# A Mamba and mixture-of-experts layer on one core: a quarter of the scan's input products move from VectorE to ScalarE and TensorE

## The chip, the core and the metric

The kernel runs on one core of a Trainium2 chip. The core has TensorE (PE in the profile, its weight loads PEld), VectorE (DVE), ScalarE (ACT), GpSimd (POOL) and a sync engine (SP) that issues DMAs. The metric is the device time in microseconds. Three runs of the kernel before took 1241.63, 1243.11 and 1251.92 us.

## The reference

For 8 sequences of 512 tokens with 128 features, x is normalised and fed to two branches, whose results are added to x:

```python
xn = _layernorm(x, axis=-1)
x = x + attn(xn) + ffn(xn)
# attn: two directions (the second on the reversed sequence), each
u = silu(causal_conv(x_part) + b)                 # 256 channels
delta = softplus(dt_proj @ x_dbl[:r] + dt_bias)   # (d, l)
dA  = exp(delta[d, l] * A[d, n])                  # 16 states n
dBx = delta[d, l] * Bm[n, l] * u[d, l]
h   = scan over l of  h = dA * h + dBx
y   = sum over n of h * Cm[n, l]  + D * u;  y * silu(z)
# attn result: (forward + backward) @ out_proj
# ffn: top 4 of 16 experts per token, softmax of the 4 logits as weights,
hidden = gelu(x @ w1[e].T + b1[e]);  hidden @ w2[e].T + b2[e]
```

All is float32.

## The kernel before, in words

**Preparation.** The first 275 us or so normalise the tokens, route them to experts (DVE), scatter them to tiles of 256 rows in DRAM (POOL), and compute for each of the 8 batches (sequences) delta, du = delta * u, the gate, and Bm and Cm, all stored to DRAM. Bm is kept as three bf16 parts in `parts`, so that a bf16 matmul with 0/1 weights `sel` sums them to the f32 value.

**The scan loop.** Channels lie on the 128 partitions; there are 256 channels, so NH = 2 halves h, and ND = 2 directions d. A batch has PAIRS = 32 steps q. Step q handles half h = q % 2 of direction d = q // 2 % 2, for the pair of states 2g and 2g + 1 with g = q // 4 (j = 0 and 1). For each of the 64 (q, j) of a batch:

- PE broadcasts row n of Bm over all partitions into one of four PSUM banks `b_ps` (L1007; called a fill).
- DVE multiplies the bank by du in place (`dbx`, L1235, the input product).
- ACT computes the decay exp(delta * A) (L829) into a ring of 8 steps.
- DVE runs the scan over 512 positions (L1257), into the ring `state` of 8 steps.

Then for each q the state times Cm (a 128x1024 product, the state product) is done by POOL (L666), or by DVE (L1245) for the steps of `vector_pairs(b)`: 4 steps in the first batch, 5 in the last and one in the others. PE adds the products up by transposing them into `y_ps` (L954, eight transposes a step, `sum_states`), four steps later (SUM_LAG).

**The experts beside it.** 10 tiles a batch are worked off in the same loop, at fixed steps (`EVENTS`, with `FIRST` and `LAST` for the first and last batch). Of tile j, T transposes the rows (L968), U0 and U1 are the first matmuls (L975), D is the second with its bias (L982 and L984, the bias as a matmul of one row of ones), G and O turn and project the gated output of the batch before. They share two PSUM banks `m_ps`; ACT empties them (L769, L773, L779, L782) at a step of its own that is 4 to 6 later (`EMPTY_STEP`), and runs the gelus in two bursts of five a batch, at its steps 5 and 21 (L797, with table loads before and after). POOL sends each finished tile to DRAM by scatter-add (`send`, L651, two indirect DMAs) one step after its D.

**The order.** Each engine runs one program in order, written out by hand, with semaphores between them. ACT's decays can run 8 steps ahead of DVE's scans. PE's fill for tau = 2q + j waits for the scan of tau - 4. PE does at step q: two fills, the events, the sum of step q - 4. The scan of q waits for the sum of q - 8. SP loads Cm rows, weights and the next batch's data in a fixed order, behind waits on the products.

```python
for j in range(2):
    tau = 2 * q + j
    if tau + 1 < DECAYS:
        dbx(tau + 1)
    ...
    nc.vector.tensor_tensor_scan(state[:, q % H_RING, j, way], ...)
```

Of the kernel before, what the change touches and what calls it, by code (L numbers as in the profile page):

```python
# [6 lines left out]
BF16 = mybir.dt.bfloat16  # L7
# [6 lines left out]
P = 128  # L14
# [45 lines left out]
FIRST_VECTOR = (1, 4, 7, 10)  # L60
VECTOR = (16,)
LAST_VECTOR = (16, 19, 22, 25, 28)
# [7 lines left out]


# [19 lines left out]
GATE_STEP, MIX_STEP = 3, 16  # L91
# [4 lines left out]
FIRST = [[] for _ in range(PAIRS)]  # L96
# [14 lines left out]
for _k, (_q, _j, _before) in enumerate(LAST_D):  # L111
    LAST[_q].append(("D", _j, 1 if _q < LAST_U[-1] else _k % 2, _before))
for _j, _q in enumerate(LAST_T):
    LAST[_q].append(("T", _j, 0, False))
for _j, _q in enumerate(LAST_U):
    LAST[_q] += [("U0", _j, 1, False), ("U1", _j, 0, False)]
# [42 lines left out]
def uses_before(b, m):  # L159

    if isinstance(b, int) and b == 0:
        return 0
    if isinstance(b, int) and b == BATCH:
        return uses_before(BATCH - 1, m) + sum(e[2] == m for q in LAST for e in q)
    return sum(e[2] == m for q in EVENTS for e in q) * b - sum(e[2] == m and e[3] for q in EVENTS for e in q)

# [51 lines left out]
def build_kernel(nc, x_in, consts_in, chan_in, inw_in, xproj_in, dtw_in, outw_in,  # L218
                 route_in, b2_in, w1_in, w2_in, out):
    with ExitStack() as ctx:  # L220
# [33 lines left out]

        delta = sb("delta", [P, 2, DH, L])
# [10 lines left out]
        b2 = sb("b2", [P, W_RING, D])  # L266
        ones = sb("ones", [P, P])
# [5 lines left out]
        ARENA = (DA_RING + H_RING + C_RING) * 2 * L + MPB * FC * S  # L273
# [3 lines left out]
        def carve(n):  # L277
# [5 lines left out]
        decay = carve(DA_RING * 2 * L).rearrange("p (r j l) -> p r j l", r=DA_RING, j=2)  # L283
        state = carve(H_RING * 2 * L).rearrange("p (r j l) -> p r j l", r=H_RING, j=2)
        c_rows = carve(C_RING * 2 * L).rearrange("p (r j l) -> p r j l", r=C_RING, j=2)
        hidden = carve(MPB * FC * S).rearrange("p (t f s) -> p t f s", t=MPB, f=FC)
# [54 lines left out]
        xpad = carve(NH * PADL).rearrange("p (h l) -> p h l", h=NH)  # L341
        v = by_q(carve(DH * L))
        u = [by_q(carve(DH * L)) for _ in range(2)]
        xdbl = by_d(carve(ND * L))
# [16 lines left out]
        b_ps = ps[:, 0:B_RING, :]  # L361
# [11 lines left out]
            late_in1 skip_in0 skip_in1 decay_ready b_ready dbx_done scan_done prod_done v_prod_done summed y_free m0_ready m0_free m1_ready m1_free gelu_done  # L373
            mixed_out mixed_in sp_step pool_step acc_ready out_done"""
# [27 lines left out]
        def _(sp):  # L402
# [6 lines left out]
            for dst, src in ((chan[:, :, :], chan_in), (inw, inw_in), (xproj, xproj_in), (dtw[BR:BR + NR], dtw_in),  # L409
# [3 lines left out]
                with nc.allow_non_contiguous_dma(reason="one row of biases"):  # L413
                    sp.dma_start(dst, src).then_inc(s["wts_in"], 16)

# [44 lines left out]
            def read_down(tile, slot):  # L460
# [3 lines left out]
                sp.dma_start(b2[0:1, slot, :], b2_in[bass.ds(e, 1)]).then_inc(w2_in_s[slot], 16)  # L464
# [13 lines left out]
            def read_first():  # L478

                sp.wait_ge(s["scattered"], 16 * NT * TOPK)  # L480
                for j in range(W_RING):
# [23 lines left out]

            store_gate(0)
# [11 lines left out]
            def read_c(b, r):  # L518
                g, d = r // ND, r % ND
                src = c_d[bass.ds(b, 1), d, 2 * g:2 * g + 2, :].rearrange("e j l -> e (j l)")  # L520
                sp.dma_start(c_rows[:, r % C_RING, :, :].rearrange("p j l -> p (j l)"),
# [26 lines left out]
            def batch(b, par):  # L548
                last = isinstance(b, int) and b == BATCH - 1
                for q in range(PAIRS + 2):  # L550
                    if q == 0 and not last:

                        wait(sp, s["decay_ready"], DECAYS * b)
                        wait(sp, s["dbx_done"], DECAYS * b)
                        wait(sp, s["b_ready"], DECAYS * b)
# [30 lines left out]
            sp.wait_ge(s["mixed_out"], 16 * (BATCH - 1))  # L586
            half = BATCH // 2
# [27 lines left out]
        def _(pool):  # L615
# [4 lines left out]
            nc.gpsimd.iota(xn[:, :, D].bitcast(I32), [[L, BATCH], [1, TPB]], base=UNUSED, channel_multiplier=TPB).then_inc(s["ids_ready"], 1)  # L620

# [61 lines left out]
        def _(act):  # L683
# [75 lines left out]
            for b in range(BATCH):  # L759
                prepare(b)  # L760
            act.wait_ge(s["decay_free"], 1)

            def empty(b, q):
# [576 lines left out]
```

## Time and profile before

| | |
|---|---|
| median of three runs | 1243.11 us |
| profiled execution, its time | 1242.92 us |
| its span | 1240.0 us |
| instructions | 20530 |
| busy: DVE / PE / POOL / ACT | 1131.2 / 996.3 / 985.2 / 809.9 us |
| first and last scan start | 279.9, 1200.1 us |
| PE weight loads busy | 748.6 us |

Times in the rows are microseconds from the start of the span, unless marked ns. A busy engine is one with an instruction in flight; two records of one engine can overlap, since the next begins before the last has quite ended. What an instruction costs in a full queue is therefore the distance from start to start. Idle time is put down to what ended it.

### The profile page before, as it was taken

The page shows a single profiled execution, that of the slowest core. Times are in us where ns is not written, and L with a number is a line of the kernel's source. Part 1 is how long each engine was busy: PE and PEld are TensorE (multiplying, and loading weights), DVE is VectorE, ACT ScalarE, POOL GpSimd, SP SyncE. Part 2 cuts the span into 40 slices and gives each one's busy share as a digit, 9 for nine tenths or more (in the row PEclk, how much of TensorE's full clock was granted, in tenths as well). Part 3 has the DMA queues.
Part 4 walks back from the last instruction along what each step waited for, and adds up shares of the span by engine and source line. Part 5 has one row for each costly group of instructions (what it writes and reads, how often), then busy time and mean ns, then how long its engine had stood idle before and what let it go on. Part 6 is the DMA issues. An engine that isn't in the chain of part 4 may idle for free.

```text
span 1240.0 us, 20530 instructions
## 1 busy us (share of the span) xinstructions
PE 996.3 (80%) x5548; PEld 748.6 (60%) x5636; DVE 1131.2 (91%) x1516; ACT 809.9 (65%) x1367; POOL 985.2 (79%) x540
## 2 busy tenths in 40 slices
PE   5277888645789888988998889899889888998972
PEld 5133333213567677776777677677667776777762
DVE  6876888759999999999999999999999999998972
ACT  2047877855677676767677676667676776767520
POOL 1077868763489989998999898799989998997673
PEclk9988787776999999999999998999999999999886
DMA  9824455486556767576676667566765666655545
GB/s 318 299 83 168 164 202 183 174 295 219 158 158 152 196 184 186 157 214 172 146 210 175 178 153 215 141 177 164 210 184 146 206 177 169 171 145 151 127 102 148
DMA packets 150908, 222.52 MB, mean 179 GB/s; under 512 B 35597, under 2 KB 97373, under 8 KB 145893
## 3 DMA queue, kind: packets, MB, share of 16 engines
q1 hardware_dynamic: 123652, 202.12, 51.7%
q0 software_dynamic: 27136, 19.02, 10.8%
q8 instruction: 49, 0.80, 0.3%
q14 instruction: 71, 0.57, 0.2%
HBM read 159.71 MB, written 65.50 MB: 182 GB/s over the span
## 4 chain that ended last, share of the span: by engine, by line
issue 37%; DVE 32%; PE 14%; POOL 7%; DMA 5%; ACT 3%; DVEq 1%; another core or an unknown queue 1%; SPq 0%; POOLq 0%; ACTq 0%
DVE ps L1235 20%; DVE arena L1257 7%; POOL arena L666 4%; POOL acc_d L651 3%; DMA acc_d<-yrows,tags 3%; PE ps L909 2%; PE ps L885 2%; PE ps L917 2%; PE ps L894 2%; PE ps L975 1%; PE ps L954 1%; PE ps L982 1%; PE ps L867 1%; ACT arena L829 1%; PE ps L1007 1%
## 5 line engine op out<-in xcount | busy, mean ns | idle before, releaser
L666 POOL TENSOR_TENSOR arena<-arena 128x1024 f32<-128x1024 f32 x241 | 608.2, 2832 | 85.3 <-DVE arena L1257 73.9
L1257 DVE TENSOR_TENSOR_SCAN arena<-arena,ps 128x512 f32<-128x512 f32 x512 | 617.7, 1208 | 0.0
L829 ACT ACTIVATE arena<-delta,a_neg 128x511 f32<-128x511 f32 x512 | 336.9, 719 | 39.2 <-DVE arena L1257 28.3
L1235 DVE TENSOR_TENSOR ps<-du,ps 128x512 f32<-128x512 f32 x512 | 344.1, 673 | 14.2 <-remote 9.8
L651 POOL DMA_INDIRECT acc_d<-yrows,tags x160 | 252.3, 1577 | 45.0 <-issue 36.7
L954 PE MATMUL ps<-ident,arena 128*128 128x128 f32 x2048 | 275.1, 279 | 0.0
L1007 PE MATMUL ps<-parts,sel 128*128 128x512 bf16 x425 | 154.9, 392 | 118.2 <-DVE arena L1257 101.5
L954 PEld LDWEIGHTS ps<-ident,arena 128*128 128x128 f32 x2048 | 236.9, 144 | 17.4 <-issue 0.8
L982 PE MATMUL ps<-w,arena 128*128 128x128 f32 x1280 | 184.6, 288 | 6.0 <-ACT yrows L779 5.6
L633 POOL DMA_INDIRECT slots_d<-arena,pos x128 | 155.8, 1217 | 42.1 <-issue 40.7
L779 ACT ACTIVATE yrows<-ps,tags 128x128 f32<-128x128 f32 x160 | 49.9, 363 | 197.6 <-PE ps L984 148.9
L982 PEld LDWEIGHTS ps<-w,arena 128*128 128x128 f32 x1280 | 160.1, 194 | 26.1 <-issue 8.0
L773 ACT ACTIVATE arena<-ps,w 128x256 f32<-128x256 f32 x320 | 131.4, 471 | 46.4 <-PE ps L975 41.8
L975 PE MATMUL ps<-rowsT,w 128*128 128x256 f32 x640 | 157.5, 390 | 1.6 <-issue 0.9
L1007 PEld LDWEIGHTS ps<-parts,sel 128*128 128x128 bf16 x512 | 50.2, 98 | 164.0 <-DVE arena L1257 149.1
L975 PEld LDWEIGHTS ps<-rowsT,w 128*128 128x128 f32 x640 | 124.6, 196 | 26.6 <-issue 3.5
L797 ACT ACTIVATE arena<-arena 128x1024 f32<-128x1024 f32 x80 | 81.1, 1053 | 0.2
L984 PE MATMUL ps<-b,ones 1*128 1x128 f32 x320 | 78.6, 325 | 0.0
L1150 DVE SCALAR_TENSOR_TENSOR arena<-arena,chan 128x512 f32<-128x512 f32 x96 | 64.3, 743 | 0.0
L984 PEld LDWEIGHTS ps<-b,ones 1*128 1x128 f32 x320 | 47.6, 186 | 19.7 <-issue 0.9
L630 POOL COPY arena<-gates 128x32 f32<-128x32 f32 x4 | 7.2, 1808 | 64.5 <-DVE pos L1123 56.1
L885 PE MATMUL ps<-arena 128*128 128x256 f32 x64 | 28.6, 625 | 33.5 <-ACT arena L701 26.9
(122 smaller groups left out, 831.3 us busy)
## 6 DMA issues: line engine op xcount, KB each, us to landing
arena<-c_d SPq DMA_DIRECT2D x128, 512.0 KB
w<-w_dram SPq DMA_DIRECT2D x80, 258.0 KB
w<-w_dram SPq DMA_DIRECT2D x80, 256.0 KB
rows<-slots_d SPq DMA_DIRECT2D x80, 130.0 KB
slots_d<-delta SPq DMA_DIRECT2D x5, 2015.0 KB, 20.1
delta_d<-arena SPq DMA_DIRECT2D x8, 1024.0 KB
du_d<-delta SPq DMA_DIRECT2D x8, 1024.0 KB
delta<-delta_d SPq DMA_DIRECT2D x8, 1024.0 KB, 6.9
```

What stands on the lines that cost most here:

```text
L633: pool.indirect_dma_start(slots_d, bass.IndirectOffsetOnAxis(ap=pos[:, t * TOPK + k:t * TOPK + k + 1], axis=0), xn[:, t, :], None).then_in ...
L651: pool.indirect_dma_start(acc_d, bass.IndirectOffsetOnAxis(ap=tags[:, j, a, 0:1].bitcast(I32), axis=0), yrows[:, j % W_RING, a, :], None, ...
L666: nc.gpsimd.tensor_tensor(state[:, q % H_RING], state[:, q % H_RING], c_rows[:, r % C_RING], ALU.mult).then_inc(s["prod_done"], 1)
L773: last = nc.scalar.activation(hidden[:, j, c, :], bank[:, f * S:(f + 1) * S], ACT.Identity, bias=w1[:, j % W_RING, FF + c:FF + c + 1])
L829: nc.scalar.activation(decay[:, q % DA_RING, j, lo:lo + L - 1], delta[:, par, dh, lo:lo + L - 1], ACT.Exp, scale=a_neg[:, dh, 2 * g + j:2 ...
L954: last = nc.tensor.matmul(y_ps[:, h, t * P:(t + 1) * P], state[:, q % H_RING, j, t * P:(t + 1) * P], ident[:, :], is_transpose=True, start ...
L975: last = nc.tensor.matmul(bank[:, f * S:(f + 1) * S], w1[:, slot, c * P:(c + 1) * P], rowsT[:, :], start=True, stop=True)
L982: nc.tensor.matmul(bank[:, a * P:(a + 1) * P], hidden[:, j, c, a * P:(a + 1) * P], w2[:, slot, c, :], start=c == 0, stop=False)
L984: last = nc.tensor.matmul(bank[:, a * P:(a + 1) * P], ones[0:1, :], b2[0:1, slot, :], start=False, stop=True)
L1007: nc.tensor.matmul(b_ps[:, tau % B_RING, :], sel[:, 2 * g + j, :], parts[:, par, d, :], start=True, stop=True).then_inc(s["b_ready"], 1)
L1235: nc.vector.tensor_tensor(bank, du[:, par, tau // 2 % DH, :], bank, ALU.mult).then_inc(s["dbx_done"], 1)
L1257: nc.vector.tensor_tensor_scan(state[:, q % H_RING, j, way], decay[:, q % DA_RING, j, way], b_ps[:, tau % B_RING, way], 0.0, ALU.mult, ALU ...
```

## The change

Of the input products, those with d = 0 and j = 1 (`scaled(q, j)`, 16 of 64 a batch) are no longer made by DVE. du of a batch's forward direction is transposed once (positions on partitions) into `duT`, and so is Bm into `bT`. For each group g ACT multiplies four 128x256 blocks of `duT` by the per-partition scalar `bT[:, t, n]` into `scaled_du` (a ring of 2), and PE transposes them into the PSUM bank, four transposes a fill. The transposing of the next batch is two new kinds of events, X (du, one half each) and Y (Bm), at steps 18 and 19.

Where a fill is still a broadcast row, it is made once for both halves: for even q DVE reads the row in one bank of its j and writes the product to the other; for odd q it works in place. Five fills are left for four steps (`FILLS`), six input products on DVE (`DBX`). The order of DVE's instructions is written out for groups of four steps.

State products on DVE become 3, 3 and 8 in the first, the middle and the last batch. Expert bias b2 is split into three bf16 parts by POOL at the start, stored to DRAM, and added by a bf16 matmul of three rows. `hidden` shrinks from ten slots to five (two more in the last batch lie in `delta`). The steps of T and D in the last batch shift a little.

```diff
-FIRST_VECTOR = (1, 4, 7, 10)
-VECTOR = (16,)
-LAST_VECTOR = (16, 19, 22, 25, 28)
+FIRST_VECTOR = (1, 4, 7)
+VECTOR = (8, 16, 24)
+LAST_VECTOR = (13, 16, 18, 20, 22, 24, 26, 28)
...
+def scaled(q, j):
+    return q // NH % ND == 0 and j == 1
+FILLS = [(q, j) for q in range(PAIRS) for j in (1, 0) if scaled(q, j) or q % NH == 0]
+DBX = [(q, j) for g in range(0, PAIRS, DH) for q, j in ((g, 0), (g + 1, 0), (g + 2, 1), (g + 2, 0), (g + 3, 0), (g + 3, 1))]
+def fill_of(q, j):
+    return 1 + FILLS.index((q, j) if scaled(q, j) else (q - q % NH, j))
...
+SCAN_ORDER = [(0, 1), (0, 0), (1, 1), (1, 0), (2, 1), (2, 0), (3, 0), (3, 1)]
+def scans_to(q, j):
+    return 2 * DH * (q // DH) + SCAN_ORDER.index((q % DH, j)) + 1
+PROD_RING = 2
+PROD_AHEAD = 2
+SCALED = PAIRS // DH
...
+EVENTS[18] += [("X", 0, 0, False), ("Y", 0, 1, False)]
+EVENTS[19].insert(0, ("X", 1, 0, False))
...
-LAST_T = [0, 3, 5, 8, 10, 12, 15, 17, 20, 22]
-LAST_U = [1, 4, 6, 9, 11, 13, 16, 18, 21, 23]
-LAST_D = [(2, 5, True), (5, 6, True), (7, 7, True), (10, 8, True), (12, 9, True), (17, 0, False), (19, 1, False),
+LAST_T = [0, 2, 4, 7, 9, 12, 15, 17, 20, 22]
+LAST_U = [2, 4, 6, 9, 11, 13, 16, 18, 21, 23]
+LAST_D = [(1, 5, True), (3, 6, True), (5, 7, True), (8, 8, True), (10, 9, True), (17, 0, False), (19, 1, False),
...
@@ SP
-                sp.dma_start(b2[0:1, slot, :], b2_in[bass.ds(e, 1)]).then_inc(w2_in_s[slot], 16)
+                sp.dma_start(b2[0:3, slot, :], b2_d[bass.ds(e, 1)].rearrange("e k d -> (e k) d")).then_inc(w2_in_s[slot], 16)
...
+            sp.wait_ge(s["b2_split"], 4)
+            sp.dma_start(b2_d.rearrange("e k d -> e (k d)"), b2_parts.rearrange("e k d -> e (k d)")).then_inc(s["b2_out"], 16)
             store_gate(0)
...
@@ POOL
+            pool.wait_ge(s["b2_in"], 16)
...
+            nc.gpsimd.tensor_copy(b2_parts[:, 0, :], b2_f).then_inc(s["b2_split"], 1)
...
@@ ACT
+            act.wait_ge(s["turn_ps"], 3)
+            act.wait_ge(s["du_ready"], ND * (BATCH - 1))
+            for h in range(NH):
+                nc.scalar.copy(duT[:, 0, :, h * P:(h + 1) * P], ps[:, h, :].rearrange("p (t c) -> p t c", t=TPB)).then_inc(s["turned"], 1)
+            nc.scalar.copy(bT[:, 0, :, :].rearrange("p t n -> p (t n)"), ps[:, 2, 0:TPB * NS]).then_inc(s["turned"], 1)
+            def scale(b, g, par):
+                n = 2 * g + 1
+                before = fill_of(DH * ((g - PROD_RING) % SCALED) + NH - 1, 1)
+                wait(act, s["b_ready"], len(FILLS) * (b if g >= PROD_RING else b - 1) + before)
+                for t in range(TPB):
+                    last = nc.scalar.activation(scaled_du[:, g % PROD_RING, t, :], duT[:, par, t, :], ACT.Identity,
+                                                scale=bT[:, par, t, n:n + 1])
+                last.then_inc(s["scaled"], 1)
...
+                    if (q + PROD_AHEAD) % DH == 0:
+                        g = (q + PROD_AHEAD) // DH
+                        if g < SCALED:
+                            scale(b, g, par)
+                        elif not (isinstance(b, int) and b == BATCH - 1):
+                            for what, j, m in (("X", 0, 0), ("X", 1, 0), ("Y", 0, 1)):
+                                bank_emptied(act, s, b, what, j, m)
+                            scale(b + 1, 0, 1 - par)
...
@@ PE
+            def turn_du(bank, par, h):
+                for t in range(TPB):
+                    last = nc.tensor.transpose(bank[:, t * P:(t + 1) * P], du[:, par, h, t * P:(t + 1) * P], ident[:, :])
+                return last
...
+            pe.wait_ge(s["delta_ready"], ND * BATCH)
+            pe.wait_ge(s["turned"], 3)
...
-                            last = nc.tensor.matmul(bank[:, a * P:(a + 1) * P], ones[0:1, :], b2[0:1, slot, :], start=False, stop=True)
+                            last = nc.tensor.matmul(bank[:, a * P:(a + 1) * P], ones[0:3, :], b2[0:3, slot, :], start=False, stop=True)
...
+                    for j in (1, 0):
+                        if (q, j) in FILLS:
+                            wait(pe, s["scan_done"], DECAYS * b + scans_to(q - 2, j))
+                            if scaled(q, j):
+                                pe.wait_ge(s["scaled"], SCALED * b + g + 1)
+                                bank = b_ps[:, ROW[q, j], j, :]
+                                for t in range(TPB):
+                                    last = nc.tensor.transpose(bank[:, t * P:(t + 1) * P],
+                                                               scaled_du[:, g % PROD_RING, t, h * P:(h + 1) * P], ident[:, :])
+                            else:
+                                last = nc.tensor.matmul(b_ps[:, ROW[q + 1, j], j, :], sel[:, 2 * g + j, :], parts[:, par, d, :],
+                                                        start=True, stop=True)
+                            last.then_inc(s["b_ready"], 1)
...
@@ DVE
+                def dbx(q, j):
+                    dve.wait_ge(s["b_ready"], len(FILLS) * b + fill_of(q, j))
+                    if q % NH == 0:
+                        wait(dve, s["scan_done"], DECAYS * b + scans_to(q - 1, j))
+                    b_row = b_ps[:, ROW[q - q % NH + 1, j], j, :]
+                    nc.vector.tensor_tensor(b_ps[:, ROW[q, j], j, :], du[:, par, q % DH, :], b_row, ALU.mult)\
+                        .then_inc(s["dbx_done"], 1)
...
+                for q in range(0, PAIRS, DH):
+                    dbx(q, 0)
+                    product(q - 1)
+                    scan(q, 1)
+                    scan(q, 0)
+                    dbx(q + 1, 0)
+                    product(q)
+                    scan(q + 1, 1)
+                    scan(q + 1, 0)
+                    dbx(q + 2, 1)
+                    product(q + 1)
+                    dbx(q + 2, 0)
+                    scan(q + 2, 1)
+                    dbx(q + 3, 0)
+                    scan(q + 2, 0)
...
+                    dbx(q + 3, 1)
+                    product(q + 2)
+                    scan(q + 3, 0)
+                    scan(q + 3, 1)
```

## Rows read from the trace of the kernel before

**Rows 1.** The page, busy microseconds, share of the span and instructions of each engine.

```profile
PE 996.3 (80%) x5548; PEld 748.6 (60%) x5636; DVE 1131.2 (91%) x1516; ACT 809.9 (65%) x1367; POOL 985.2 (79%) x540
```

**Rows 2.** Stretches: length, busy of PE, PEld, DVE, ACT, POOL; granted clock, DMA share, GB/s.

```profile
406.60:518.40 111.80, 97.73 (x641) 80.26 (x652) 111.77 (x133) 80.77 (x152) 104.10 (x52) 1.00 0.68 180
...
743.80:860.50 116.70, 103.79 (x645) 83.49 (x653) 114.25 (x133) 81.39 (x154) 102.72 (x52) 0.96 0.67 175
```

**Rows 3.** Timeline of DVE in a middle batch: start, length, engine, line, operation, operands.

```profile
638.92 1.21 DVE L1257 TENSOR_TENSOR_SCAN arena<-arena,ps 128x512 f32<-128x512 f32 x1
640.04 0.67 DVE L1235 TENSOR_TENSOR ps<-du,ps 128x512 f32<-128x512 f32 x1
...
664.54 1.21 DVE L1257 TENSOR_TENSOR_SCAN arena<-arena,ps 128x512 f32<-128x512 f32 x1
```

**Rows 4.** Timeline of DVE at the end of the first batch.

```profile
393.49 2.32 DVE L1257 TENSOR_TENSOR_SCAN arena<-arena,ps 128x512 f32<-128x512 f32 x2
```

**Rows 5.** The group of L1245, then timelines of DVE and POOL around three of its instructions.

```profile
L1245 DVE TENSOR_TENSOR arena<-arena 128x1024 f32<-128x1024 f32 x15 | 24.6, 1643 | 1.0
...
679.57 1.23 DVE L1245 TENSOR_TENSOR arena<-arena 128x1024 f32<-128x1024 f32 x1
...
795.00 2.94 POOL L666 TENSOR_TENSOR arena<-arena 128x1024 f32<-128x1024 f32 x1
795.61 3.42 DVE L1245 TENSOR_TENSOR arena<-arena 128x1024 f32<-128x1024 f32 x1
...
1188.34 3.27 DVE L1245 TENSOR_TENSOR arena<-arena 128x1024 f32<-128x1024 f32 x1
```

**Rows 6.** Timeline of the last batch and the tail; in brackets the idle time before.

```profile
1128.43 2.77 PE L994 MATMUL ps<-outw,gatedT 128*128 128x128 f32 x16 [3.45 <-ACT gatedT L782]
...
1133.45 0.70 DVE L1235 TENSOR_TENSOR ps<-du,ps 128x512 f32<-128x512 f32 x1 [4.15 <-remote]
...
1200.41 0.62 ACT L779 ACTIVATE yrows<-ps,tags 128x128 f32<-128x128 f32 x2 [9.95 <-DMA acc_d<-yrows,tags]
```

**Rows 7.** Timeline of POOL in a middle batch: a send, three products, the next send.

```profile
645.53 1.60 POOL L651 DMA_INDIRECT acc_d<-yrows,tags  x1 [0.17 <-issue]
647.44 1.57 POOL L651 DMA_INDIRECT acc_d<-yrows,tags  x1 [0.30 <-issue]
648.44 7.59 POOL L666 TENSOR_TENSOR arena<-arena 128x1024 f32<-128x1024 f32 x3
656.20 1.58 POOL L651 DMA_INDIRECT acc_d<-yrows,tags  x1 [0.16 <-issue]
```

**Rows 8.** Timeline of PE and ACT at a batch's step 18, behind the gelu burst.

```profile
679.80 1.15 PE L982 MATMUL ps<-w,arena 128*128 128x128 f32 x8
...
680.20 1.33 ACT L829 ACTIVATE arena<-delta,a_neg 128x511 f32<-128x511 f32 x2
682.99 0.62 ACT L779 ACTIVATE yrows<-ps,tags 128x128 f32<-128x128 f32 x2 [1.45 <-PE ps L984]
...
685.71 1.70 ACT L773 ACTIVATE arena<-ps,w 128x256 f32<-128x256 f32 x4 [0.89 <-PE ps L975]
```

**Rows 9.** Groups of one middle batch (518.4 to 630.3): busy, mean ns, idle before.

```profile
L666 POOL TENSOR_TENSOR arena<-arena 128x1024 f32<-128x1024 f32 x32 | 81.2, 2885 | 3.1 <-DVE arena L1257 3.1
...
L954 PE MATMUL ps<-ident,arena 128*128 128x128 f32 x256 | 33.7, 275 | 0.0
...
L984 PE MATMUL ps<-b,ones 1*128 1x128 f32 x40 | 9.7, 321 | 0.0
L779 ACT ACTIVATE yrows<-ps,tags 128x128 f32<-128x128 f32 x20 | 6.2, 363 | 23.1 <-PE ps L984 18.6 <-issue 4.4
```

**Rows 10.** Timeline of PE: two fills in a row.

```profile
649.14 0.59 PE L1007 MATMUL ps<-parts,sel 128*128 128x512 bf16 x2
```

**Rows 11.** Timeline of ACT at the start of the scan loop.

```profile
276.66 12.33 ACT L829 ACTIVATE arena<-delta,a_neg 128x511 f32<-128x511 f32 x20 [8.51 <-DVE arena L1198]
```

**Rows 12.** Stretches, as in rows 2, of seven microseconds in the fifth batch.

```profile
758.00:765.00 7.00, 6.78 (x24) 5.64 (x25) 5.34 (x7) 2.57 (x6) 6.44 (x4) 0.55 0.74 182
```

More of the change, by code:

```diff
@@ L69, in vector_pairs @@
     return VECTOR
+def scaled(q, j):
[4 more added lines that the diff above has]
+    return 1 + FILLS.index((q, j) if scaled(q, j) else (q - q % NH, j))
+ROW = {}
+for _j in range(2):
+    _last = 1
+    for _q in range(0, PAIRS, NH):
+        ROW[_q, _j], ROW[_q + 1, _j] = (1 - _last, _last) if scaled(_q, _j) else (_last, 1 - _last)
+        _last = ROW[_q + 1, _j]
+    assert _last == 1 and NH == 2
+SCAN_ORDER = [(0, 1), (0, 0), (1, 1), (1, 0), (2, 1), (2, 0), (3, 0), (3, 1)]
[4 more added lines that the diff above has]
+SCALED = PAIRS // DH
 SUM_LAG = 4
@@ L373, in build_kernel @@
             late_in1 skip_in0 skip_in1 decay_ready b_ready dbx_done scan_done prod_done v_prod_done summed y_free m0_ready m0_free m1_ready m1_free gelu_done
+            b2_in b2_split b2_out turn_ps turned scaled
             mixed_out mixed_in sp_step pool_step acc_ready out_done"""
@@ L586, in _ @@
             sp.wait_ge(s["mixed_out"], 16 * (BATCH - 1))
+            for j in (GROUP, GROUP + 1):
+                m = [e[2] for step in LAST for e in step if e[:2] == ("D", j) and not e[3]][0]
+                bank_written(sp, s, BATCH - 1, "D", j, m)
             half = BATCH // 2
@@ L782, in empty @@
                         last = nc.scalar.copy(gatedT[:, j, :], bank)
+                    elif what == "X":
+                        last = nc.scalar.copy(duT[:, 1 - par, :, j * P:(j + 1) * P], bank.rearrange("p (t c) -> p t c", t=TPB))
+                    elif what == "Y":
+                        last = nc.scalar.copy(bT[:, 1 - par, :, :].rearrange("p t n -> p (t n)"), bank[:, 0:TPB * NS])
                     else:
@@ L988, in besides @@
                             last = nc.tensor.transpose(bank[:, t * P:(t + 1) * P], gated[:, j, t, :], ident[:, :])
+                    elif what in ("X", "Y"):
+                        pe.wait_ge(s[f"early_in{1 - par}"], 48 * (i + par) + 48)
+                        last = turn_du(bank, 1 - par, j) if what == "X" else turn_b(bank, 1 - par)
                     else:
@@ new lines, in dbx, with scan @@
+                def dbx(q, j):
[5 more added lines that the diff above has]
+                        .then_inc(s["dbx_done"], 1)
+                def scan(q, j):
+                    dve.wait_ge(s["decay_ready"], DECAYS * b + 2 * q + j + 1)
+                    if scaled(q, j):
+                        dve.wait_ge(s["b_ready"], len(FILLS) * b + fill_of(q, j))
+                    else:
+                        dve.wait_ge(s["dbx_done"], len(DBX) * b + DBX.index((q, j)) + 1)
+                    wait(dve, s["summed"], PAIRS * b + q - H_RING + 1)
+                    way = slice(None) if q % DH < NH else slice(None, None, -1)
+                    nc.vector.tensor_tensor_scan(state[:, q % H_RING, j, way], decay[:, q % DA_RING, j, way],
+                                                 b_ps[:, ROW[q, j], j, way], 0.0, ALU.mult, ALU.add).then_inc(s["scan_done"], 1)
```

125 lines of the change are left out of this document (72 added, 53 removed).

## The prediction

> **What bounds the kernel now.** I read the page's busy line first: VectorE (DVE) is busy 91% of the span, more than any other engine [rows 1]. The table by stretches then separates the stages: from 406.6 us on, a batch of the scan loop takes 111.9 us, in which DVE is busy 111.8, POOL 104.1, PE 99 and ACT 81 [rows 2]. DVE waits for nobody in such a batch, so what a batch costs is what DVE's instructions cost. The timeline of DVE gives their real price, from start to start, as records overlap: 15 pairs of an input product (L1235) and a scan (L1257) lie between the first and the last row shown, 25.62 us or 1.708 a pair; the scan's part is 1.12 to 1.13 and so the product's 0.58 [rows 3]. 64 pairs are 109.3, one state product on DVE 1.15, two gate products 1.2: 111.7 of the 111.9. The profiled execution took 1242.92 us, its span 1240.0, and the median of the three runs is 1243.11, so the sum made against the profiled one holds for the median too.
>
> **DVE, what goes.** A quarter of the input products (those of d = 0, j = 1: 16 of 64 a batch) leave DVE: 16 x 0.58 = 9.3 us a batch. The new order puts scan behind scan; two adjacent scans are recorded once a batch end, 2.32 us for both, so the second starts 1.11 after the first, no dearer than 1.13 [rows 4]. An even q now reads its row in one bank and writes another; the nearest row is the in-place product at 0.58. It could cost a little more or less; I take the same, since the shape and memories are those of L1235.
>
> **DVE, what comes.** State products move from POOL to DVE: 3 a batch in place of 1, 3 in place of 4 in the first, 8 in place of 5 in the last. One alone takes 1.23 us (slot 1.15), as at 679.57 where POOL was issuing a send. At 795.61 it took 3.42: POOL was inside its own product from 795.00 to 797.94, and the DVE product ended 1.1 us after that. At 1188.34, 3.27 in the same way. The mean of the 15 is 1.643 [rows 5]. So the slot lies between 1.15 and 3.35. The clean ones fell on sends or on an idle POOL; with three a batch at places not tied to a send and POOL inside a product 0.64 of the time (29 x 2.34 of 107), half of a product's 2.34 is the mean wait: 0.64 x 1.17 = 0.75, so 1.9 a slot. The Trainium skill, page "SBUF — State Buffer", section "SBUF: two separate sides", says that a DVE instruction with two inputs in SBUF and a GpSimd one that reads SBUF take one port pair as an exclusive lock for the whole instruction. The trace agrees, with 3.42 against 1.23 us. Without a lock, each product at 1.15, the sum would be 1185; the rule speaks against the change's extra products, not against its scaled ones (one input of L1235 is PSUM, and it never stretched).
>
> **The sum for DVE.** A middle batch: 48 x 0.58 + 64 x 1.125 = 99.8; gate 1.2; three products 5.7; 106.7 in all. For brief stalls of a now tighter loop I add 0.8 (0 to 4 would be the bounds, the latter from the one stall of the last batch [rows 6]), so 107.5 against 111.9: 4.4 saved, x 6 = 26. First batch: 9.3, and one product fewer among idle or light POOL, +0.8, less 0.6 as the first fill now stands behind four transposes: 9.5. Last batch: 9.3 + 8.6 (the five old products: 1.2, 1.2, 1.2, 1.7, 3.3) - 15.2 (eight at 1.9) = 2.7. The tail after 1201 us hangs on the scatter-adds: ACT waits 9.95 us for a send to land before it may fill the next slot [rows 6]; nothing of it changes, and it moves with the last batch. 26 + 9.5 + 2.7 = 38: 1242.9 - 38 = 1205.
>
> **POOL.** Three products make 7.02 us between the ends of the last send and of the third product, 2.34 each; a send takes the other 3.61 of a 10.63 us cycle [rows 7]. Now 31 x 2.34 + 10 x 3.61 = 108.6 a batch; after, 29 x 2.34 + 36.1 = 104.0, plus up to 3 x 1.15 where DVE holds what POOL wants: 104 to 107.4. It is nearly level with DVE. Sends come in stretches, so POOL falls behind by some 4 us over eight steps and gets it back at the DVE products; PE's sum is four steps behind, which covers about 6.
>
> **ACT.** Added are 32 ACTIVATEs of 128x256 a batch. Four such from PSUM take 1.70, 0.41 each; from SBUF they lie between 0.41 and the 0.61 of a 511-wide decay, two of which take 1.33 [rows 8]; I take 0.41: 13.1, and 1.4 for the turned copies. 81 + 14.5 = 95.5 of 107.5. It fits beside DVE because ACT's 23 us of idle before L779 in a batch are mostly waits for PE's D, which ACT reaches early [rows 9]. Its cover gone, each us above costs one us of loop. The scale is issued two steps ahead and its ring of two is refilled against transposes five steps older, so it waits for nobody.
>
> **PE.** Two fills in a row take 0.59, 0.3 each [rows 10]; 40 fewer save 12. L954's 256 transposes keep PE busy 33.7 us, 0.13 each [rows 9]; 64 more are 8.4, and with a start-up for each group of four 10. The biases in f32 take 9.7 a batch [rows 9]; in bf16 with three rows something between 0 and that; I take 4.7: 5 saved. X and Y add 12 small ones, 1.6. Net 5 less: 94 of 107.5. But PE is in order, and X and Y put two new waits for ACT at steps 18 and 19 behind which the fills of step 20 stand. PE began D of step 18 at 679.80, ACT was through its gelu burst at 680.20 and emptied D at 682.99 [rows 8]. From there: Y, X copies, X, U0, U1, two sums and the fills of 20 come to about 9 us from the start of D; DVE has 6 scans, 5 input products and one state product to do, 11.5. It just fits.
>
> **Start and queues.** Transposing batch 0 and the three copies fall in the idle time before the first decays, 8.5 us of ACT up to 276.66 [rows 11], which wait for DVE's last preparation; some 4 us of work there, cost 0, at most 3 if the load of du comes late. The split of b2 is four small POOL instructions ahead of its wait for pos, which DVE computes much later: 0. On SP's queue the store of b2 and the extra waits (b2_split ahead of the first gate store, products 8 and 24) are passed long before the rest is due: 0, at most 1.
>
> **Rivals.** (a) POOL sets the pace: 107.4 plus the 3.1 us that it still waits for scans in a batch [rows 9] is 110.5, 1.4 saved x 6, + 12: 1222. For it: 104 to 107 against 106.7 leave no room. (b) The new waits park PE as ACT's late copy did in the last batch: PE waited 3.45 us, DVE 4.15 [rows 6]. Once in each of 7 batches: 1205 + 29 = 1234. (c) Slower: ACT becomes the bound, because its waits for PE's D don't shrink as it falls behind. Then a batch is 95.5 + 23.1 = 118.6, + 6.7 x 6 - 9.5: 1273. It decides once more than 16.4 of the 23.1 us stay. Against it: ACT is up to eight steps ahead, and such waits end at PE's time. (d) Products hit POOL's sends and nothing stalls: 104.5 a batch, 7.4 x 6 + 10.5 + 8.7: 1179. (e) PE's clock. Between 758 and 765 us PE was granted 0.55, a fall to its lower level, 1.2 GHz, right after ordinary busy work; that batch took 116.7 [rows 2, 12]. One such stretch in each of 7 batches: 1205 + 33 = 1238. The Trainium skill, "TensorE: Matmul & The Clock Gate", part 4, says that transposes don't count as busy for the clock, and this change swaps matmuls for transposes. The trace is against it so far: a steady batch with 256 transposes of L954 alone holds 1.00 [rows 2, 9]. (f) The change does less than it says, DVE still running 512 input products: 1243. The diff leaves six of eight in each group of four steps, so this gets 2%.
>
> **Chances.** Forecast 0.50, (a) 0.14, (b) 0.09, (c) 0.11, (d) 0.11, (e) 0.03, (f) 0.02. A measurement of this kernel can tell about 1%, 12 us: faster is below 1231, slower above 1255. Faster: 0.50 + 0.14 + 0.11 less some for overlap of (a) with the border: 0.73. Within: 0.15. Slower: 0.12. The bounds of the product slot alone give 1179 (1.15) and 1242 (3.35); (a) and (b) lie between, (c) is left out. Range 1180 to 1238.
>
> **What would show it.** Right: scans in a middle batch stay unbroken, gates 107 to 108 us apart, 384 input products on DVE, 29 state products of mean 1.7 to 2.2 us, PE's waits at fills for scans still there. Wrong: DVE idle before L1257's or L1235's successors released by PE (b), by ACT decays (c), or scans held by sums behind POOL (a); granted clock under 0.9 in a middle batch (e).

## The result: 1% slower, and the profile after

The changed kernel took 1252.1 us in the median of five runs (1248.43 to 1265.39) against 1241.6 for the kernel before; the ratio is 1.0107, with a 95% interval of 1.006 to 1.0154. The forecast of 1205 us was wrong. Run again beside its variants it took 1255.42 against 1244.61, ratio 1.0097 (1.0064 to 1.013). Now and then a run of a kernel takes 1.5% or more longer than its shortest; where that matters below, its time is named beside the others.

The profiled execution of the changed kernel is the slowest of its five, 1265.39 us with a span of 1263.5, so I use it for the pattern and not for the sum. Its busy line answers [rows 1]:

```profile
PE 981.4 (78%) x5764; PEld 781.2 (62%) x5764; DVE 1087.3 (86%) x1402; ACT 915.4 (72%) x1647; POOL 874.1 (69%) x530
```

DVE did get rid of work: 44 us less. But it is now busy 86% of the span, no longer 91%. The table by stretches, cut at the gate products as in [rows 2], shows the same in a middle batch:

```profile
409.10:523.10 114.00, 96.78 (x668) 84.42 (x668) 107.69 (x118) 94.03 (x187) 89.39 (x49) 0.96 0.64 174
...
873.50:989.50 116.00, 98.26 (x668) 85.47 (x668) 107.81 (x119) 94.07 (x188) 89.37 (x49) 0.94 0.65 173
```

DVE's work of a batch is 107.7 us, where I had 106.7. The six middle batches take 114.0 to 119.7, so 6 to 12 us of each are waits; the first batch of [rows 2] had none. POOL's 89.4 is far below my 104. The page's groups say who waits, and for whom (line, engine, operands, count; then busy and mean ns; then the idle time before and its releasers):

```profile
L747 POOL TENSOR_TENSOR arena<-arena 128x1024 f32<-128x1024 f32 x227 | 486.9, 2241 | 219.4 <-DVE arena L1389 208.4
L1389 DVE TENSOR_TENSOR_SCAN arena<-arena,ps 128x512 f32<-128x512 f32 x512 | 600.9, 1205 | 1.2 <-ACT arena L932 1.2
L1377 DVE TENSOR_TENSOR ps<-du,ps 128x512 f32<-128x512 f32 x384 | 254.7, 678 | 50.3 <-PE ps L1146 47.9
...
L854 ACT ACTIVATE arena<-arena 128x256 f32<-128x256 f32 x256 | 108.7, 497 | 36.8 <-PE ps L1143 36.8
...
L1096 PE MATMUL ps<-ident,rows 128*128 128x128 f32 x160 | 35.4, 306 | 85.2 <-ACT arena L872 84.8
```

L1389 is the scan, L1377 the input product, L1146 and L1143 the fills (row and transposes), L854 the new scaling, L1096 the transposing T of an expert tile, L872 ACT's emptying of U0 and U1. Read upwards it is a chain: ACT stands before the scaling until PE has made certain transposes, PE stands 85 us before T until ACT has emptied U1, and DVE stands before its input products until PE has filled. Also DVE waits at the gate products (L1365):

```profile
873.47 0.67 DVE L1365 TENSOR_TENSOR gated<-ps,gate 128x512 f32<-128x512 f32 x1
...
877.84 0.69 DVE L1365 TENSOR_TENSOR gated<-ps,gate 128x512 f32<-128x512 f32 x1 [3.71 <-PE ps L1082]
```

The timeline around step 29 of a batch shows how one such meeting goes (start, length; idle before in brackets):

```profile
849.40 0.60 PE L1143 MATMUL ps<-ident,arena 128*128 128x128 f32 x4
...
850.04 1.71 ACT L854 ACTIVATE arena<-arena 128x256 f32<-128x256 f32 x4 [2.87 <-PE ps L1143]
...
851.65 1.54 ACT L872 ACTIVATE arena<-ps,w 128x256 f32<-128x256 f32 x4
...
853.25 0.44 PE L1096 MATMUL ps<-ident,rows 128*128 128x128 f32 x2 [3.25 <-ACT arena L872]
...
854.86 1.29 DVE L1377 TENSOR_TENSOR ps<-du,ps 128x512 f32<-128x512 f32 x2 [2.05 <-PE ps L1146]
```

ACT had been idle for 2.87 us when PE made the transposes of step 29 (L1143); only then could it scale (1.6 us) and only then empty U1 (1.6 us). PE needs that bank for T of the same step 29, so it stood 3.25 us, which is the two together. DVE ran out of filled rows and stood 2.05. This is the dearest of several meetings: in the whole trace ACT waits before the scaling 16 times, twice in a middle batch, but PE waits before T behind L872 34 times. So a part of PE's 84.8 us has no wait of ACT's before it.

### The profile page after: what moved, and what is told of

It reads as the page before. It is cut to its first block, busy times and chain, and to the rows that moved or that the text cites. A ratio compares the mean times of both kernels' runs of the same rounds, so it can differ in the third digit from the quotient of the medians.

```text
span 1263.5 us, 21454 instructions
## 1 busy us (share of the span) xinstructions
PE 981.4 (78%) x5764; PEld 781.2 (62%) x5764; DVE 1087.3 (86%) x1402; ACT 915.4 (72%) x1647; POOL 874.1 (69%) x530
## 4 chain that ended last, share of the span: by engine, by line
issue 17%; PE 16%; ACT 15%; POOL 10%; DVE 4%; DMA 3%; DVEq 0%; SPq 0%; ACTq 0%; POOLq 0%
POOL arena L747 5%; POOL acc_d L732 5%; PE ps L1111 5%; PE ps L1082 4%; ACT arena L932 4%; ACT arena L854 3%; ACT arena L872 3%; PE ps L1103 3%; DVE arena L1389 2%; ACT arena L900 2%; DMA acc_d<-yrows,tags 2%; PE ps L1143 2%; DVE ps L1377 1%; ACT L932 1%; PE ps L1146 1%
## 5 line engine op out<-in xcount | busy, mean ns | idle before, releaser
L747 POOL TENSOR_TENSOR arena<-arena 128x1024 f32<-128x1024 f32 x227 | 486.9, 2241 | 219.4 <-DVE arena L1389 208.4
L1389 DVE TENSOR_TENSOR_SCAN arena<-arena,ps 128x512 f32<-128x512 f32 x512 | 600.9, 1205 | 1.2 <-ACT arena L932 1.2
L1377 DVE TENSOR_TENSOR ps<-du,ps 128x512 f32<-128x512 f32 x384 | 254.7, 678 | 50.3 <-PE ps L1146 47.9
L1082 PE MATMUL ps<-ident,arena 128*128 128x128 f32 x2048 | 285.8, 285 | 2.9 <-POOL arena L747 2.9
L1082 PEld LDWEIGHTS ps<-ident,arena 128*128 128x128 f32 x2048 | 245.5, 148 | 16.7 <-POOL arena L747 3.4
L1111 PEld LDWEIGHTS ps<-w,arena 128*128 128x128 f32 x1248 | 169.7, 208 | 22.6 <-ACT yrows L878 7.2
L878 ACT ACTIVATE yrows<-ps,tags 128x128 f32<-128x128 f32 x160 | 49.6, 361 | 128.4 <-PE ps L1113 95.2
L872 ACT ACTIVATE arena<-ps,w 128x256 f32<-128x256 f32 x312 | 125.8, 468 | 19.7 <-PE ps L1103 18.5
L854 ACT ACTIVATE arena<-arena 128x256 f32<-128x256 f32 x256 | 108.7, 497 | 36.8 <-PE ps L1143 36.8
L1143 PE MATMUL ps<-ident,arena 128*128 128x128 f32 x512 | 84.5, 292 | 24.3 <-DVE arena L1389 18.5
L1096 PE MATMUL ps<-ident,rows 128*128 128x128 f32 x160 | 35.4, 306 | 85.2 <-ACT arena L872 84.8
L1146 PE MATMUL ps<-parts,sel 128*128 128x512 bf16 x192 | 71.3, 415 | 25.4 <-DVE arena L1389 25.4
L1143 PEld LDWEIGHTS ps<-ident,arena 128*128 128x128 f32 x512 | 64.3, 151 | 28.5 <-DVE arena L1389 21.8
L1096 PEld LDWEIGHTS ps<-ident,rows 128*128 128x128 f32 x160 | 19.8, 149 | 99.9 <-ACT arena L872 86.6
```

What stands on the lines that cost most here:

```text
L747: nc.gpsimd.tensor_tensor(state[:, q % H_RING], state[:, q % H_RING], c_rows[:, r % C_RING], ALU.mult).then_inc(s["prod_done"], 1)
L854: last = nc.scalar.activation(scaled_du[:, g % PROD_RING, t, :], duT[:, par, t, :], ACT.Identity, scale=bT[:, par, t, n:n + 1])
L872: last = nc.scalar.activation(hidden[hidden_slot(b, j)][:, c, :], bank[:, f * S:(f + 1) * S], ACT.Identity, bias=w1[:, j % W_RING, FF + c: ...
L1082: last = nc.tensor.matmul(y_ps[:, h, t * P:(t + 1) * P], state[:, q % H_RING, j, t * P:(t + 1) * P], ident[:, :], is_transpose=True, start ...
L1111: nc.tensor.matmul(bank[:, a * P:(a + 1) * P], kept[:, c, a * P:(a + 1) * P], w2[:, slot, c, :], start=c == 0, stop=False)
L1143: last = nc.tensor.transpose(bank[:, t * P:(t + 1) * P], scaled_du[:, g % PROD_RING, t, h * P:(h + 1) * P], ident[:, :])
```

## The experiments

Theory R: the wait of the scaling on the ring of two, at the place where the change has it, holds ACT back to PE's own step. Rival L: ACT simply has too much to do. Rival G: the wait at the gate is a cost of its own. Rival O: the new order of fills and products leaves PE too little lead. The ratios are to the kernel before, timed beside each.

**The yardstick.** 

> The changed kernel once more, as the yardstick for its variants on the same chip. All theories: about 1.01 of the kernel before, DVE idle some 45 us before L1377 (released by PE's fills) and 33 us before the gate products in the loop, PE idle some 85 us before T (L1096) behind ACT's emptying of U1.

1255.42 us; in its profile DVE is idle 45.0 us before L1377 and 40.6 before L1365, 13.0 of these in the tail; PE is idle 85.8 before T behind L872, as expected of it.

**The scaling at its own step.**

```diff
-PROD_AHEAD = 2
+PROD_AHEAD = 0
...
-                        if g < SCALED:
+                        if g > 0:
                             scale(b, g, par)
-                        elif not (isinstance(b, int) and b == BATCH - 1):
+                        elif not (isinstance(b, int) and b == 0):
                             for what, j, m in (("X", 0, 0), ("X", 1, 0), ("Y", 0, 1)):
-                                bank_emptied(act, s, b, what, j, m)
-                            scale(b + 1, 0, 1 - par)
+                                bank_emptied(act, s, b - 1, what, j, m)
+                            scale(b, 0, par)
```

> ACT issues the four scaling instructions of group g at its step 4g and not at 4g - 2, so the ring of two is refilled against transposes that PE did seven steps earlier, not five. Theory R (the ring's wait holds ACT up, ACT empties U1 late, PE stands before T, DVE waits): ACT's 37 us of idle before L854 fall below 10, PE's 85 us before T below 45, time 1220 to 1235. Rival L (ACT's plain load of 14 us a batch makes it late): the waits before T stay at 70 to 90 us and the time within 6 us of the changed kernel. Rival G (the gate's position): no change in the 33 us before the gate products.

1202.54 us, ratio 0.9657 (0.9605 to 0.9709): 53 us below the changed kernel with the same instructions, by their place alone. That is further than the 1220 to 1235 that R had said; the two waits fell as R had them. The groups of its whole profile, in the same order:

```profile
L1377 DVE TENSOR_TENSOR ps<-du,ps 128x512 f32<-128x512 f32 x384 | 252.9, 673 | 14.1 <-issue 5.6 <-remote 4.5 <-PE ps L1143 3.7
L854 ACT ACTIVATE arena<-arena 128x256 f32<-128x256 f32 x256 | 108.9, 505 | 0.0
L1096 PE MATMUL ps<-ident,rows 128*128 128x128 f32 x160 | 32.9, 288 | 28.7 <-ACT arena L872 21.2 <-DMA tags<-slots_d 5.8 <-DVE arena L1389 0.6
```

ACT's idle before the scaling is 0.0, PE's before T behind L872 a quarter, and DVE's before the input products a third. The timeline around a step 29 of this kernel shows the meeting gone:

```profile
805.48 1.70 ACT L872 ACTIVATE arena<-ps,w 128x256 f32<-128x256 f32 x4
...
807.02 0.60 PE L1143 MATMUL ps<-ident,arena 128*128 128x128 f32 x4
...
807.41 2.31 DVE L1389 TENSOR_TENSOR_SCAN arena<-arena,ps 128x512 f32<-128x512 f32 x2
807.45 0.38 PE L1096 MATMUL ps<-ident,rows 128*128 128x128 f32 x2
...
809.64 0.67 DVE L1377 TENSOR_TENSOR ps<-du,ps 128x512 f32<-128x512 f32 x1
...
810.99 1.70 ACT L854 ACTIVATE arena<-arena 128x256 f32<-128x256 f32 x4
```

ACT empties U0 and U1 from 805.48 on, before PE's transposes; PE makes T 0.43 us after it has begun the transposes, without a wait in brackets; the scaling comes 4 us later, after the emptying and not before it, and DVE shows no wait either. The table by stretches, again from gate to gate, for two of the six middle batches:

```profile
610.10:721.60 111.50, 94.84 (x668) 81.52 (x675) 107.93 (x118) 96.77 (x193) 89.98 (x50) 0.98 0.68 183
829.00:936.30 107.30, 92.92 (x662) 81.02 (x669) 107.30 (x119) 94.04 (x187) 89.33 (x50) 0.98 0.71 188
```

In the second DVE is busy for the whole of the batch. Four of the six are like it, 107.3 to 107.8 us, the 107.5 that I had forecast; the other two take 111.5 and 110.7. ACT's work is as large as before the repair, 94.04, so rival L, that ACT's sum is too large wherever it stands, is out. The gate products are recorded as one unbroken pair in six of seven batches, and DVE's idle time before them falls from 40.6 to 21.9 us, 12.2 of it one wait in the tail; G had them unchanged.

**The gate in halves.**

```diff
                     if q == 0 and not first:
-                        gate_batch(b - 1, 1 - par, i if par else i - 1)
+                        gate_batch(b - 1, 1 - par, i if par else i - 1, (0,))
...
                     dbx(q, 0)
+                    if q == DH and not first:
+                        gate_batch(b - 1, 1 - par, i if par else i - 1, (1,))
                     product(q - 1)
```

> The gate product of the second half moves from behind the scan of (2, 0) to behind the first input product of step 4, where PE has already done the sum that it needs; all else as changed. Theory G (the gate's wait is a cost of its own): the 3.5 us before it go in 7 batches, 25 us less, about 1228. Theories R and L (PE is late because of ACT, the gate is only where DVE meets it first): DVE then waits for the fills of step 4 or later in its place, and the time falls by less than 8 us.

1248.12 us, ratio 1.0037 (1.0004 to 1.0069), 7 us below the yardstick, inside the 8 us of R and L; G had 25. Its DVE row:

```profile
L1377 DVE TENSOR_TENSOR ps<-du,ps 128x512 f32<-128x512 f32 x384 | 254.8, 678 | 58.8 <-PE ps L1146 29.5 <-PE ps L1143 21.8 <-remote 5.4
```

The gate's idle fell by 18 us, that before the input products rose by 14. The wait moved, as R and L have it.

**Everything but the scaling.**

```diff
 def scaled(q, j):
-    return q // NH % ND == 0 and j == 1
+    return False
-DBX = [... ((g, 0), (g + 1, 0), (g + 2, 1), ...)]
+DBX = [... ((g, 0), (g, 1), (g + 1, 0), (g + 1, 1), (g + 2, 1), ...)]
-EVENTS[18] += [("X", 0, 0, False), ("Y", 0, 1, False)]
-EVENTS[19].insert(0, ("X", 1, 0, False))
...
+                    dbx(q, 1)
...
+                    dbx(q + 1, 1)
```

> Everything of the change but the scaling: DVE makes all 64 input products of a batch, from rows shared by both halves; no X, no Y, no scaling on ACT; three, three and eight state products on DVE, bias in bf16. By the slots a middle batch is 64 x 0.58 + 72.0 + 1.2 + 3 x 1.9 = 116 us without any wait, so about 1270 in all. Theories R and L (what ACT was given causes the waits): DVE idle in the loop under 12 us, PE's before T under 15, 1262 to 1278. Rival O (the new order of fills and products leaves PE too little lead, whatever ACT does): DVE still idle 40 us or more, over 1290.

1265.31 us, ratio 1.0137 (1.0077 to 1.0196), inside the expected band. Its input product (L1366) waits little:

```profile
L1366 DVE TENSOR_TENSOR ps<-du,ps 128x512 f32<-128x512 f32 x512 | 329.2, 676 | 7.5 <-issue 4.4 <-PE ps L1135 3.0
```

Between 290 and 1195 us DVE is idle 19.0 us in all, more than the 12 expected and half of the 40 that O asked for; the time is below O's 1290. So O is out as the main cause. Against the own-step kernel, the scaling itself is worth 63 us (60 by the ratios). Its 29 state products cost less than in the other variants, though:

```profile
L1386 DVE TENSOR_TENSOR arena<-arena 128x1024 f32<-128x1024 f32 x29 | 37.8, 1305 | 0.0
```

Against 24.6 us for the 15 of before [rows 5] that is 13 us more, of the 17 to 21 that this kernel is slower; the rest is not accounted for. The price of such a product depends on where it falls against POOL's [rows 5].

**A quarter of the scaling.**

```diff
-                for t in range(TPB):
+                for t in range(TPB if isinstance(b, int) and b == 0 and g < 2 else 1):
                     last = nc.scalar.activation(scaled_du[...
```

> The changed kernel with one scaling instruction of four left in each group (the rest of the block keeps old values, so part of the scaled products is left out); its waits and its place are unchanged. It takes 9.8 us of ACT's work out of a batch and leaves the wait for the transposes of two groups before. Theory R (the wait where it stands is what costs): the 37 us of idle before L854 stay or grow, PE's waits before T stay over 50 us, and the time stays above 1225. Rival L (ACT's load): time at 1205 or below, like that of the kernel with the scaling at its own step.

The four runs took 1210.27, 1213.99, 1229.45 and 1243.02 us: median 1221.72, ratio 0.9838 (0.9727 to 0.9949). Neither R (above 1225) nor L (1205 or below) said the median or the two shortest. The groups of the page of the execution that took 1210.27 us:

```profile
L854 ACT ACTIVATE arena<-arena 128x256 f32<-128x256 f32 x70 | 34.5, 500 | 34.1 <-PE ps L1143 34.1
L1096 PE MATMUL ps<-ident,rows 128*128 128x128 f32 x160 | 33.6, 293 | 51.4 <-ACT arena L872 45.9 <-DVE arena L1389 2.8 <-DMA tags<-slots_d 2.2
```

The idle before L854 stayed, 34.1 us, as R had it. PE's before T fell to 45.9 behind L872, where R had it above 50, and the two shortest runs lie 41 to 45 us below the changed kernel with the wait still there. So R put too much on the wait alone. Three instructions of 0.4 us are gone from each group, and the T of step 29 waits 1.2 us less, as the table below shows: what PE pays at a meeting is the wait and the scaling that stand ahead of the emptying, together.

**One step ahead.**

```diff
-PROD_AHEAD = 2
+PROD_AHEAD = 1
```

> The scaling issued one step ahead: six steps behind the transposes that it waits for, between five (changed kernel, 1255) and seven (own step, 1202.5). Theory R: ACT's lead over PE is five to six steps, so most of the wait goes, idle before L854 under 15 us, and the time lies between, 1202 to 1230. If it was not this wait but something else about the place: as the changed kernel, 1245 or more.

1211.32 us (1200.65 to 1212.05, and one run of 1283.59), ratio 0.9714 (0.9615 to 0.9813), in the band. The same two groups:

```profile
L854 ACT ACTIVATE arena<-arena 128x256 f32<-128x256 f32 x256 | 108.6, 499 | 0.0
L1096 PE MATMUL ps<-ident,rows 128*128 128x128 f32 x160 | 32.9, 288 | 51.6 <-ACT arena L872 48.0 <-DMA tags<-slots_d 2.2 <-DVE arena L1389 0.6
```

The wait before L854 is gone. PE still stood 48.0 us before T behind L872, twice the own-step kernel's, yet little of it reached DVE (17.6 us before L1377). The timelines of PE in one middle batch show which meetings were left. Here is the idle time of PE before T behind L872, for the T's of steps 23, 26, 29 and 3 of the next batch (that of step 0 does not wait there), with the time of the execution:

| kernel | 23 | 26 | 29 | 3 | us |
|---|---|---|---|---|---|
| changed | 2.14 | 1.86 | 3.24 | 3.20 | 1252.34 |
| a quarter of the scaling | 0.95 | 0.67 | 2.06 | 2.02 | 1210.27 |
| one step ahead | 2.14 | 1.86 | none | 1.27 | 1210.59 |
| own step | 0.55 | 0.27 | none | 1.27 | 1200.75 |

```profile
841.31 0.44 PE L1096 MATMUL ps<-ident,rows 128*128 128x128 f32 x2 [3.24 <-ACT arena L872]
...
813.25 0.44 PE L1096 MATMUL ps<-ident,rows 128*128 128x128 f32 x2 [2.06 <-ACT arena L872]
```

These are the T's of step 29 in the first two kernels. One step ahead changes nothing at 23 and 26 and takes the ring's wait out of 29 and 3; the quarter shortens all four. Each of the two gets most of the 53 us back, so the wait on the ring (none here, 34.1 us there) does not order the times by itself. What sets the changed kernel apart from the other three is the lateness at steps 29 and 3, over 3 us at each. What the last step gained, 8 to 9 us, is at the edge of what these runs tell apart.

**Own step and gate in halves** (both edits above).

> The scaling at its own step (1202.5 us) and the second gate product moved behind the first input product of step 4. If the gate still waits once ACT is on time, up to 3 us a batch go: 1185 to 1200. If its wait was only PE's lateness behind ACT: 1200 to 1205.

1204.58 us, ratio 0.9707 (0.9641 to 0.9773): nothing on top, the second case.

**Own step without X and Y** (the events and their waits removed, `duT[:, 0]` and `bT[:, 0]` read for all batches).

> The scaling at its own step (1202.5 us), without the events X and Y: batches after the first scale the turned data of batch 0, so du and Bm of the later batches are left out of those products. It prices the new events. If they park PE even with ACT on time (my rival b, 4 us a batch): 1175 or less. If they fit beside the rest, as I forecast: within 6 us of 1202.5.

1199.01 us, ratio 0.9661 (0.9597 to 0.9725), 3.5 us less by the medians and nothing by the ratios: with the scaling at its own step, X and Y fit beside the rest, and rival (b) is out. In the changed kernel itself they were not taken out.

**The state products back to POOL**, first in the changed kernel, then with the scaling at its own step.

```diff
-FIRST_VECTOR = (1, 4, 7)
-VECTOR = (8, 16, 24)
-LAST_VECTOR = (13, 16, 18, 20, 22, 24, 26, 28)
+FIRST_VECTOR = (1, 4, 7, 10)
+VECTOR = (16,)
+LAST_VECTOR = (16, 19, 22, 25, 28)
```

> The changed kernel (scaling two steps ahead) with the state products on DVE back to 4, 1 and 5. In the own-step kernel this gave 22 us. Theory R (in the changed kernel DVE waits for a PE that waits for ACT): what DVE is spared mostly turns into longer waits for fills and gates, and the time falls by 0 to 12 us from 1255. If DVE's work were the bound there too: 22 us or more, 1233.

> The scaling at its own step, and the state products on DVE back to 4, 1 and 5. DVE is the bound of the own-step kernel: by 1.94 us for each product, 2 less in each of 6 batches and 3 less in the last give 29 us, less 2 in the first: 1175, if POOL holds 31 x 2.0 + 36 = 98 us a batch beside DVE's 102. If POOL's share of the loop is again the bound (its older 2.34 a product and the sums that wait for it): 1200 or more.

1248.74 us (ratio 1.0064, 1.0022 to 1.0106) and 1180.76 us (0.9518, 0.945 to 0.9585). The same edit gave 7 us where DVE waits and 22 where DVE is the bound (by the ratios 4 and 17). For the second I had expected 29, to 1175, with 1.94 us for each product. It fell short because the products that are left got dearer:

```profile
L1397 DVE TENSOR_TENSOR arena<-arena 128x1024 f32<-128x1024 f32 x15 | 36.2, 2416 | 1.3 <-DMA arena<-c_d 1.3
```

The one in each middle batch took 3.0 to 3.7 us, where it had taken 1.23 in five of six batches of the kernel before. The first of the two kernels has 15 of the products and more idle time before its input products than the changed kernel's 50.3:

```profile
L1377 DVE TENSOR_TENSOR ps<-du,ps 128x512 f32<-128x512 f32 x384 | 254.4, 677 | 57.9 <-PE ps L1146 55.7 <-issue 2.0
```

**None in the middle batches** (as the last, with `VECTOR = ()`).

> The scaling at its own step and no state product on DVE in the middle batches (4 in the first, 5 in the last). DVE is spared the last one, 2.3 us with its wait for POOL, in each of 6 batches; POOL has 32 x 2.0 + 36 = 100 us of about 101. If DVE stays the bound: 1168 from 1181. If POOL becomes it and the sums wait: 1181 or more.

1170.82 us, ratio 0.9443 (0.938 to 0.9505), the best of all, 2.8 us off the expected 1168. Its POOL group:

```profile
L747 POOL TENSOR_TENSOR arena<-arena 128x1024 f32<-128x1024 f32 x247 | 532.3, 2449 | 89.2 <-DVE arena L1389 73.6 <-DMA arena<-c_d 15.4
```

POOL still waits 73.6 us for scans, so even here it is not the bound.

**The layout, in the kernel before.**

```diff
+        PAD = 150
-        ARENA = (DA_RING + H_RING + C_RING) * 2 * L + MPB * FC * S
+        ARENA = (DA_RING + H_RING + C_RING) * 2 * L + MPB * FC * S + PAD
...
+        top[0] += PAD
         c_rows = carve(C_RING * 2 * L)...
```

> The kernel before with 600 bytes of padding between the state ring and the Cm rows, so that the two inputs of POOL's product are no longer a multiple of 4096 bytes apart, as they are not in the changed kernel. If the distance is what made a lone product fall from 2.34 to 1.99 us: 1.99 here too, with DVE-bound time unchanged within 6 us. If something else did it: 2.34.

1239.49 us, ratio 0.9975 (0.9924 to 1.0027). The duration of POOL's product (min/median/max in ns), with the padding and without (L668 there is L666):

```profile
L668 POOL TENSOR_TENSOR arena<-arena x241: 1988/2567/2603, 283.1 to 1205.5; 128x1024 f32<-128x1024 f32 x121
```

```profile
L666 POOL TENSOR_TENSOR arena<-arena x241: 2342/2943/2978, 285.5 to 1210.1; 128x1024 f32<-128x1024 f32 x121
```

The padding alone shortens the product from 2.342 to 1.988 us at the least. In the changed kernel the two rings lie 37464 bytes apart, again 600 above a multiple of 4096, and its shortest is 1.989. So the distance is the likely cause, though the padding also moves the Cm rows and what lies behind them. The kernel's time does not show it, since DVE is the bound.

## Why the prediction was wrong, by its own steps

**DVE's sum: right.** I had 106.7 us of work in a middle batch; the trace has 107.3 to 107.9 of busy time. Where DVE is the bound four of six batches take 107.3 to 107.8, my 107.5, and the whole 1202.5, my 1205. A part of that fit is luck: from the first gate to the last the own-step kernel takes 652.1 us against 677.8 before (two of its batches stand in [rows 2]), 25.7 less and my 26, but I had counted neither that two batches before were longer (113.5 and 116.7) nor that two after would be (111.5 and 110.7). Scan behind scan, products across banks and 384 input products together cost what the rows gave.

**The state products: the mean right, partly by luck.** 29 of them, mean 1.923 us in the changed kernel and 1.943 in the own-step one, against a slot of 1.9. But I had worked the slot out from POOL's 2.34 us a product. With the 1.99 that it really takes, the same working gives 0.54 of the time inside a product, half of 1.99 as the wait, and 1.7. The mean was also 1.305 without the scaling and 2.416 for the 15 that were left with the products back and the scaling at its own step: it goes by the places where the products fall, and the share is no more than a rough guide. The longer time beside a product of POOL's shows as before. POOL's and DVE's timelines of the changed kernel:

```profile
780.85 1.58 POOL L732 DMA_INDIRECT acc_d<-yrows,tags  x1 [0.17 <-issue]
...
806.25 2.59 POOL L747 TENSOR_TENSOR arena<-arena 128x1024 f32<-128x1024 f32 x1
```

```profile
781.18 1.22 DVE L1397 TENSOR_TENSOR arena<-arena 128x1024 f32<-128x1024 f32 x1
...
807.26 2.67 DVE L1397 TENSOR_TENSOR arena<-arena 128x1024 f32<-128x1024 f32 x1
```

Beside a send the product took 1.22 us; begun 1.01 us into a product of POOL's it took 2.67, of which 1.58 passed before POOL's ended. With the scaling at its own step, 29 products on DVE cost 27 us by the ratios and 32 by the medians more than 9 (1202.5 and 1170.8), and POOL was not short of time.

**ACT: the step that failed.** "The scale is issued two steps ahead and its ring of two is refilled against transposes five steps older, so it waits for nobody." Five steps of distance are enough only if ACT leads PE by less than five. It leads by four to six, because it empties U1 of step p up to six steps later in its own program: at its step 34 (2 of the next batch) that of step 28. At that same step the scaling waits for PE's transposes of step 29, and PE's T of step 29 waits for the emptying behind the scaling. I looked at what the wait is for, and not at what is queued behind it; and I put the 1.7 us of the scaling itself, which also stand ahead of the emptying, at nothing. The place cost 53 us (1255.4 to 1202.5), 15 more than the whole gain that I had forecast. ACT's sum, 95.5 us a batch, was about right (94 to 95 in most batches). Rival (c), the only one on the slow side, was wrong in its mechanism: ACT's waits for PE's D did shrink, from 148.9 us in all to 95.2, and to 41.6 in the own-step kernel; what it did not have is the new wait of 36.8. Nor does ACT's sum decide, since the moved scaling leaves it as it was: what stands ahead of the emptying does, and the quarter of the scaling shows that both the wait and the work count.

**PE and X, Y: right.** 97 to 100 us in the changed kernel, 92 to 95 in the own-step one, where I had 94; X and Y cost at most 3.5 us in all. The 0.8 us a batch that I allowed for stalls holds for the own-step kernel alone, as a mean (none in four batches, 3.6 and 2.4 in two); in the changed one it is 6 to 12.

**POOL: mis-sized, without effect.** 2.34 us a product became 1.99 by the layout, 89.4 us a batch and not 104. Rival (a) had no chance once that is known, and no row of before could show it. (The cycle in [rows 7] is 10.67 us from start to start, not 10.63, which changes nothing.)

**The clock.** Rival (e) would have been a lost stretch of the granted clock in each batch. The changed kernel's six middle batches have 0.93 to 0.96, where five of six before had 1.00 [rows 2], and the own-step kernel's have 0.98 or 0.99. So PE was slower as well, but that is the smaller part: runs at nearly the same mean clock, 0.918 of the changed kernel and 0.919 of the own-step one, took 1250.49 and 1204.33 us, 46 apart; another pair, 0.921 and 0.916, took 1251.89 and 1206.60, 45 apart. So some 7 of the 53 us are left for the clock, an estimate from these pairs. The Trainium skill, "TensorE: Matmul & The Clock Gate", part 4, has transposes not counting as busy; the own-step kernel runs as many transposes as the changed one and holds 0.98, so that rule does not explain the difference between the two.

## What to carry to other kernels

When work is added to an engine that runs ahead of others, list for each new wait what stands behind it in that engine's program and who waits for that; a wait that is "long satisfied" by distance in the source is not so if the engine's lead is as large as the distance. Count the new work itself too, where it stands ahead of something that is waited for. Put such work as late as its consumer allows: here 0 steps ahead beat 2 by 53 us. And before moving work between engines, check which of them waits: POOL waited for DVE's scans in every variant, 74 us in all or more.

## What the runs showed of the hardware

POOL's 128x1024 product of two f32 inputs takes 2.34 us alone when its inputs lie a multiple of 4096 bytes apart, and 1.99 us when 600 bytes of padding are put between the two rings: 15% less, with no other edit to the kernel. DVE's 128x1024 product is the same in both layouts, 1.224 us at the shortest. Only these distances, and the 37464 bytes of the changed kernel, were tried.
